# Seven half-block products for the last FFN group's down projection, and VectorE pieces of the first group in another order

## What is computed

```
x = x + gated_delta(layernorm(x))   # state S = beta*S + delta*k v^T per token, K = 64, V = 128
x = x + ffn(layernorm(x))
ffn(h):  hidden = sigmoid(h Q(w1)^T) * (h Q(w2)^T)     # 512 -> 1408
         return hidden Q(w3)^T                          # 1408 -> 512
Q(w) = clip(round(w / (mean|w| + 1e-8)), -1, 1)
```

## Time and profile before

| | |
|---|---|
| median of 3 runs | 318.64 us (318.29 to 318.87) |
| profiled execution, its own time | 318.46 us |
| its span, first to last instruction | 316.7 us |
| TensorE busy | 306.8 us, 97% |
| VectorE busy | 235.2 us, 74% |
| ScalarE busy | 183.2 us, 58% |
| GpSimd busy | 177.2 us, 56% |
| chain that ended last | TensorE 64%, VectorE 11%, ScalarE 6%, DMA 5%, GpSimd 4% |

### The profile page before, as it was taken

How to read it: one execution, slowest core, us unless ns; L and a number is a source line. 1 busy time by engine, 2 the same in 40 slices (tenths; PEclk the granted TensorE clock), 3 DMA queues, 4 the chain that set the end, 5 groups by cost and what they waited for, 6 DMA issues and landing times.

```text
span 316.7 us, 7197 instructions
## 1 busy us (share of the span) xinstructions
PE 306.8 (97%) x2548; PEld 213.2 (67%) x2548; DVE 235.2 (74%) x524; ACT 183.2 (58%) x413; POOL 177.2 (56%) x419
## 2 busy tenths in 40 slices
PE   7999999999999989999999999999999999999996
PEld 5888779874544434467888744778976448888545
DVE  6879989899989898897767879669677823455401
ACT  3587986969863673624666554346655406777200
POOL 7298325589993655997334896734467302444300
PEclk9999999999999999999999999999999999999999
DMA  6999900575862156630000039200000790000011
GB/s 180 380 387 395 398 24 0 67 135 100 129 108 50 34 85 133 103 99 17 3 3 0 3 64 211 91 2 2 3 2 0 90 245 33 3 0 2 2 66 66
DMA packets 55027, 29.43 MB, mean 93 GB/s; under 512 B 46800, under 2 KB 47568, under 8 KB 54992
## 3 DMA queue, kind: packets, MB, share of 16 engines
q1 hardware_dynamic: 54672, 28.97, 36.4%
q10 hardware_dynamic: 320, 0.00, 0.1%
HBM read 13.89 MB, written 4.19 MB: 57 GB/s over the span
## 4 chain that ended last, share of the span: by engine, by line
PE 64%; DVE 11%; ACT 6%; DMA 5%; issue 5%; POOL 4%; SPq 3%; DVEq 0%; POOLq 0%; ACTq 0%
PE ffn L1638 23%; PE ffn L1620 9%; PE pd L1638 8%; PE pd L1620 8%; PE ffn L1436 5%; DVE X L1125 3%; PE lev L1512 3%; DMA x_sb<-in_L_attn_x_dram 3%; PE pd L1446 2%; ACT q L793 2%; DMA w12T<-q 2%; SPq L404 2%; DVE sc L1187 2%; PE lev L1469 1%; ACT w12T L781 1%
## 5 line engine op out<-in xcount | busy, mean ns | idle before, releaser
L1638 PE MATMUL ffn<-w_nat,w12T 128*128 128x256 f16 x468 | 63.1, 273 | 0.0
L646 POOL TENSOR_TENSOR xnT<-xnT,q 128x256 f32<-128x256 f32 x33 | 24.3, 736 | 65.5 <-ACT xnT L975 45.0
L1638 PEld LDWEIGHTS ffn<-w_nat,w12T 128*128 128x128 f16 x468 | 45.1, 98 | 8.5 <-issue 1.5
L1620 PE MATMUL ffn<-w3T,w_nat 128*128 128x512 f16 x220 | 48.3, 379 | 0.0
L1591 PE MATMUL ffn<-w_nat,w12T 128*128 128x512 f16 x176 | 39.2, 379 | 2.3 <-DVE xnT L1330 2.3
L1620 PEld LDWEIGHTS ffn<-w3T,w_nat 128*128 128x128 f16 x220 | 21.6, 98 | 25.8 <-issue 0.6
L1638 PE MATMUL ffn<-w_nat 128*128 128x256 f16 x216 | 32.4, 273 | 0.0
L1591 PEld LDWEIGHTS ffn<-w_nat,w12T 128*128 128x128 f16 x176 | 16.9, 98 | 22.7 <-issue 3.8
L1436 PE MATMUL ffn<-xnT,w_proj 128*128 128x256 f32 x128 | 29.5, 384 | 1.2 <-ACT xnT L722 0.8
L1381 DVE TENSOR_TENSOR w_nat<-xnT,w_nat 128x512 f16<-128x512 f32 x33 | 23.1, 699 | 9.1 <-ACT w_nat L983 8.5
L1365 DVE SCALAR_TENSOR_TENSOR q<-ffn,w_nat 128x256 f32<-128x256 f32 x33 | 14.0, 424 | 21.0 <-PE ffn L1638 20.9
(11 more groups left out here) (194 smaller groups left out, 642.1 us busy)
## 6 DMA issues: line engine op xcount, KB each, us to landing
x_sb<-in_L_attn_x_dram SPq DMA_DIRECT2D x16, 256.0 KB, 8.3
out_dram<-x_sb SPq DMA_DIRECT2D x15, 256.0 KB, 2.1
w_nat<-in_L_ffn_w_dram SPq DMA_DIRECT2D x2, 1536.0 KB, 12.1
w_nat<-in_L_ffn_w_dram SPq DMA_DIRECT2D x2, 1408.0 KB, 15.5
w_nat<-in_L_ffn_w_dram SPq DMA_DIRECT2D x2, 1280.0 KB, 12.9
...
```

The source lines that it names most:

```text
L646: nc.gpsimd.tensor_tensor(hid32[:, u % 2, HP:2 * HP], sig[:, u % 2, HP:2 * HP], up[:, u % 2, HP:2 * HP], ALU.mult).then_inc(pool_hid, 1)
L1620: done = nc.tensor.matmul(down_bank(g, m)[:, :], hid_at(g, part, j, m), w3T[:, j, :], start=n == 0, stop=n == 2 * HT - 1)
L1638: done = nc.tensor.matmul(out[:, 0:HP], weights[:, t, u * P:(u + 1) * P], tokens[:, part, t, :], start=first and t == 0 and part == 0, sto ...
```

## The change

**Down projection of group 3.** Of the 11 hidden tiles ten are taken as two halves of five (JD = 5), the 512 tokens as two halves (the sequences b), the 512 output columns as two halves. The 2x2 by 2x2 block product is made from seven block products instead of eight, each of 20 matmuls of 256 columns (2 token tiles, 2 parts, 5 hidden tiles), and the eleventh tile adds 16 matmuls. `down_blocks` writes out their order on TensorE.

The factors that aren't there yet are made during the loop. GpSimd makes one difference or sum of 256 columns per step behind hidden_a, in steps for u = 0 to 9; VectorE makes four f16 weight differences of 1280 columns in steps k = 2 to 5 behind up_a, and two f32 pieces of 256 columns for each of five tiles (`down_sums`) between hidden_lo and up_a in steps k = 8 to 11 (two pairs in the last). The four sums are split into f16 parts by ScalarE (`down_hi_early`, `down_hi_late`) and VectorE (`down_lo`), 1280 columns each. VectorE adds each block product to x_sb as it is done (`down_group`), and SP stores in five parts (`store_blocks`). The first five hidden tiles are kept in f32 in buffers that are free by then (keep_at). The hidden scale of the last group is 16 instead of 64.

**First group.** In the tables of group 0, norm2 and apply of chunk 2 and its splits and transposes stand one unit later, and so do two weight sums. In `product1` the wait for y_ready of u = 1 is gone for group 1.

Left out below: new semaphores, hs(g) in place of HS, hid_f32 in place of hid32, `half_block` and `rest_block` (one matmul of 256 columns each; two for the eleventh tile), `add_block` (one scalar_tensor_tensor), and the removal of `down_last` and of the halves in `add_out` and `store_y`.

```diff
-    HS = 64.0
+    HS, HS_LAST = 64.0, 16.0
+    JD = (HT - 1) // 2
...
-        DVE_NEXT_FAST = {k: v for k, v in DVE_AFTER.items() if k != "xlo"}
-        DVE_NEXT_FAST |= {"sums": (None, 12), "xlo": (8, 12), "xloS": (None, 12)}
-        ACT_NEXT_FAST = {"gt": (2, 7), "oT": (4, 9), "xhiN": (7, 12), "xhiS": (8, 12)}
+        DVE_NEXT_FAST = {"chain0": (0, 5), "chain1": (0, 5), "masks": (2, 7), "state": (4, 9), "resid": (5, 11),
+                         "norm2": (6, 11), "apply": (7, 12), "sums": (None, 12), "xlo": (9, 12), "xloS": (None, 12)}
-        ACT_NEXT_FAST = {"gt": (2, 7), "oT": (4, 9), "xhiN": (7, 12), "xhiS": (8, 12)}
+        ACT_NEXT_FAST = {"gt": (2, 7), "oT": (4, 9), "xhiN": (8, 12), "xhiS": (9, 12)}
-        SP_NEXT_FAST = {"turn": (9, 12)}
+        SP_NEXT_FAST = {"turn": (10, 12)}
-        T_AT = {4: (3,), 5: (2,), 7: (4,), HT + 2: (1,)}
+        T_AT = {4: (3,), 6: (2,), 8: (4,), HT + 2: (1,)}
...
+        keep_at = ([xs[:, b, :, :].rearrange("p s d -> p (s d)").bitcast(f32) for b in range(B)]
+                   + [w_nat[:, WN + at:WN + at + 512] for at in (XS_AT[2][1] + 640, XS_AT[2][1] + 640 + 512, T_END)])
+        dsum = [f[:, 0:JD * HP].rearrange("p (j n) -> p j n", j=JD)
+                for f in (x_all[:, :, :, :].rearrange("p a b d -> p (a b d)"),
+                          x_all[:, :, :, :].rearrange("p a b d -> p (a b d)")[:, JD * HP:2 * JD * HP],
+                          X[:, :, :].rearrange("p l n -> p (l n)"),
+                          w_proj[:, :, :, :].rearrange("p a t n -> p (a t n)"))]
+        dsplit = store[:, :, :].rearrange("p c n -> p (c n)").bitcast(f16)[:, 0:8 * JD * HP].rearrange(
+            "p (n s j m) -> p n s j m", n=4, s=2, j=JD)
+        DT1, DT2, DT3, DT4 = (w_nat[:, WN + at:WN + at + JD * P].bitcast(f16).rearrange("p (j n) -> p j n", j=JD)
+                              for at in (0, JD * P, 2 * JD * P, XS_AT[2][1]))
+        d_left, d_right = slice(0, HP), slice(HP, D)
+        d_rows, d_rest = slice(0, JD), slice(JD, 2 * JD)
...
+            return keep_at[u] if g == G - 1 and u < JD else hid32[:, u % 2, :]
...
+            return {"x": pab[0][:, t * HP:(t + 1) * HP], "y": pab[1][:, t * HP:(t + 1) * HP],
+                    "v": pco[0][:, t * HP:(t + 1) * HP], "z": (pco[1], bank[0])[t][:, 0:HP]}[name]
...
+            def store_blocks(g):
+
+                sp_.wait_ge(y_ready, g * DT + 1)
+                store_half(0, d_left, slice(2 * g, 2 * g + 2))
+                sp_.wait_ge(x_read, 3)
+                store_half(1, d_left, slice(2 * g, 2 * g + 2))
+                sp_.wait_ge(y_ready, g * DT + 2)
+                store_half(0, d_right, slice(2 * g, 2 * g + 1))
+                sp_.wait_ge(y_ready, g * DT + 3)
+                store_half(1, d_right, slice(2 * g, 2 * g + 2))
+                sp_.wait_ge(y_ready, g * DT + 4)
+                store_half(0, d_right, slice(2 * g + 1, 2 * g + 2))
...
+                if g == G - 1 and u > JD + 1:
+                    pool.wait_ge(d24_ready, u - JD - 1)
+                nc.gpsimd.tensor_tensor(hid_f32(g, u)[:, 0:HP], sig[:, u % 2, 0:HP], up[:, u % 2, 0:HP],
                                         ALU.mult).then_inc(pool_hid, 1)
+                if g == G - 1 and u < JD:
+                    pool.wait_ge(pool_hid, 2 * n + 2)
+                    nc.gpsimd.tensor_tensor(dsum[2][:, u, :], hid_f32(g, u)[:, 0:HP], hid_f32(g, u)[:, HP:2 * HP],
+                                            ALU.subtract).then_inc(d3_ready, 1)
+                if g == G - 1 and JD <= u < 2 * JD:
+                    pool.wait_ge(pool_hid, 2 * n + 2)
+                    nc.gpsimd.tensor_tensor(dsum[0][:, u - JD, :], hid_f32(g, u - JD)[:, HP:2 * HP],
+                                            hid_f32(g, u)[:, HP:2 * HP], ALU.add).then_inc(d1_ready, 1)
...
+            def down_hi_early():
+
+                act.wait_ge(d24_ready, JD)
+                nc.scalar.activation(dsplit[:, 1, 0, :, :], dsum[1], ACT.Copy).then_inc(dhi_ready, 1)
+                act.wait_ge(d1_ready, JD)
+                nc.scalar.activation(dsplit[:, 0, 0, :, :], dsum[0], ACT.Copy).then_inc(dhi_ready, 1)
+
+            def down_hi_late():
+
+                act.wait_ge(d3_ready, JD)
+                nc.scalar.activation(dsplit[:, 2, 0, :, :], dsum[2], ACT.Copy).then_inc(dhi_ready, 1)
+                nc.scalar.activation(dsplit[:, 3, 0, :, :], dsum[3], ACT.Copy).then_inc(dhi_ready, 1)
...
+                    down_hi_early()
                 hidden_hi(g, HT - 1)
+                if g == G - 1:
+                    down_hi_late()
+                    return
...
+            def down_weights(n):
+
+                left, right = w3T[:, :, d_left], w3T[:, :, d_right]
+                if n == 0:
+                    done = nc.vector.tensor_tensor(DT3, right[:, d_rest, :], right[:, d_rows, :], ALU.subtract)
+                if n == 1:
+                    done = nc.vector.tensor_tensor(DT2, DT3, left[:, d_rows, :], ALU.add)
+                if n == 2:
+                    done = nc.vector.tensor_tensor(DT4, left[:, d_rest, :], DT2, ALU.subtract)
+                if n == 3:
+                    done = nc.vector.tensor_tensor(DT1, right[:, d_rows, :], left[:, d_rows, :], ALU.subtract)
+                done.then_inc(dT_ready, 1)
+                dve.wait_ge(dT_ready, n + 1)
+
+            def down_sums(g, p):
+
+                dve.wait_ge(d1_ready, p + 1)
+                dve.wait_ge(pool_hid, 2 * fast_n(g, JD + p) + 2)
+                link(nc.vector.tensor_tensor(dsum[1][:, p, :], dsum[0][:, p, :], hid_f32(g, p)[:, 0:HP], ALU.subtract))
+                nc.vector.tensor_tensor(dsum[3][:, p, :], hid_f32(g, JD + p)[:, 0:HP], dsum[1][:, p, :],
+                                        ALU.subtract).then_inc(d24_ready, 1)
+
+            def down_lo(n, nth):
+
+                dve.wait_ge(dhi_ready, nth)
+                nc.vector.tensor_tensor(dsplit[:, n, 1, :, :], dsum[n], dsplit[:, n, 0, :, :],
+                                        ALU.subtract).then_inc(dlo_ready, 1)
+
+            def add_block(g, b, cols, name, t=None):
+
+                if t is None:
+                    y = x_sb[:, b, 2 * g:2 * g + 2, cols]
+                    part = {"x": pab[0], "y": pab[1], "v": pco[0]}[name][:, :].rearrange("p (t n) -> p t n", t=2)
+                else:
+                    y = x_sb[:, b, 2 * g + t, cols]
+                    part = d_bank(name, t)
+                return nc.vector.scalar_tensor_tensor(y, part, 1.0 / HS_LAST, y, ALU.mult, ALU.add)
+
+            def down_group(g):
+
+                dve.wait_ge(dx_done, 1)
+                add_block(g, 0, d_left, "x").then_inc(x_read, 1)
+                down_lo(1, 1)
+                hidden_lo(g, HT - 1)
+                down_lo(0, 2)
+                dve.wait_ge(dx_done, 2)
+                add_block(g, 0, d_right, "x").then_inc(x_read, 1)
+                down_lo(2, 3)
+                dve.wait_ge(dy_done, 1)
+                dve.wait_ge(x_read, 1)
+                add_block(g, 0, d_left, "y").then_inc(y_ready, 1)
+                down_lo(3, 4)
+                dve.wait_ge(dz_done, 1)
+                for t in range(2):
+                    read = add_block(g, 1, d_right, "z", t)
+                read.then_inc(z_read, 1)
+                dve.wait_ge(dv_done, 1)
+                link(add_block(g, 1, d_left, "v"))
+                dve.wait_ge(dx_done, 3)
+                add_block(g, 1, d_left, "x").then_inc(x_read, 1)
+                dve.wait_ge(dz_done, 2)
+                dve.wait_ge(x_read, 2)
+                add_block(g, 0, d_right, "z", 0).then_inc(y_ready, 1)
+                dve.wait_ge(dx_done, 4)
+                dve.wait_ge(z_read, 1)
+                add_block(g, 1, d_right, "x").then_inc(y_ready, 1)
+                dve.wait_ge(dz_done, 3)
+                add_block(g, 0, d_right, "z", 1).then_inc(y_ready, 1)
...
+                    if g == G - 1 and JD <= k - 3:
+                        down_sums(g, k - 3 - JD)
+                    if g == G - 1 and k == HT:
+                        down_sums(g, JD - 1)
                     if k > 0:
                         up_a(g, k - 1)
+                    if g == G - 1 and 2 <= k < 6:
+                        down_weights(k - 2)
...
+            def down_blocks(g):
+
+                N = 4 * JD
+                left, right = w3T[:, :, d_left], w3T[:, :, d_right]
+                product5(g, HT - 1)
+                for n in range(4):
+                    half_block("x", plain(0, 0), left[:, d_rows, :], n, True)
+                product4(g, HT - 1)
+                for n in range(4, 12):
+                    half_block("x", plain(0, 0), left[:, d_rows, :], n, True)
+                product3(g, HT - 1)
+                for n in range(12, N):
+                    done = half_block("x", plain(0, 0), left[:, d_rows, :], n, True)
+                done.then_inc(dx_done, 1)
+                pe.wait_ge(hi_ready, g * HT + 2 * JD)
```

(46 more changed lines are left out.)

90 lines of the change are left out of this document (51 added, 39 removed).

## The result

| | changed kernel | kernel before, same job |
|---|---|---|
| first measurement, 4 runs each | 321.72 us (321.25 to 321.88) | 318.71 us (318.29 to 318.87) |
| again, beside the experiments | 321.24 us (320.53 to 321.58), 5 runs | 318.83 us, 15 runs |
| ratio, first measurement | 1.0089, 95% interval 1.0077 to 1.0101 | |
| ratio, again | 1.0072, 95% interval 1.0059 to 1.0084 | |
| profiled execution | 321.82 us, span 319.8 | 318.46 us, span 316.7 |

The change makes the kernel slower, by 2.4 to 3.0 us. The forecast was 0.7 us faster, 317.9, and the range ended at 319.9: wrong in sign and outside the range.

A forecast was written before the change was run, and what follows sets the result against it. TensorE's matmuls bound the end, a VectorE, GpSimd and ScalarE chain the first group. Terms -1.99 + 0.2 + 0.49 + 0.54 = -0.76, block times -0.9; with first group +0.2: -0.7, 317.9 us, range 316.8 to 319.9.

The forecast's parts named there:

- Columns: Last down projection on TensorE: fewer columns, 19.07 us before and 17.08 after, 1.99 saved if TensorE never waits.
- Rival 4: Down projection: narrow products don't save, going by the length of one instead of by columns; 321.5 us, chance 0.02.
- GpSimd's ten pieces: Last group's loop: ten extra 256-column pieces, 0.73 us each, hidden in GpSimd's idle time; cost 0.
- dropped y_ready wait: Group 1's product1(1, 1): the wait was worth 0.4 us, but VectorE's gapless work covers it; effect 0.
- Weight differences: Last group's loop, steps 2 to 5: VectorE's pieces make hidden_a late, counted twice in four steps; +0.2, bounds 0 and 0.45.
- Ring of sums: Loop steps 8 to 11: sums delay up_a, hidden_a, hidden_hi, next hidden_lo; 3.40 us a ring; +0.49, bounds 0.29 and 1.39.
- GpSimd's late grip: Loop's sums: GpSimd takes the shared port after its record's start, an argument against hidden_b (0.25) beating the second sum (0.38).
- Block four: Down projection: TensorE waits for the split of sum 2; +0.54, bounds 0.15 and 1.2.
- Tail: After the last matmul: a 256-column add and 128 KB store as now; 0, bounds 0 and 0.3.
- First group: Second weight sum can block GpSimd's sums, delaying split, signs and chunk 3's residual add: 0.9 gained to 1.2 lost; +0.2 taken.
- the block times: Down projection's end worked out block by block: 313.2 against 314.13, so -0.9 in place of the summed terms' -0.76.
- Rival 2: Last group: hidden_b always first at the shared port; ring 1.39, block waits 1.2, weights 0.45; 319.5 to 320.3, chance 0.25.

The follow-up runs named there:

- experiment 7: Down projection's half alone, weight differences moved into group 2, sums put behind up_a one step earlier, against the kernel before: 316.76 us, ratio 0.9939.
- experiment 11: Down projection's half alone, with GpSimd's ten additional pieces cut from 256 to 16 columns: 320.58 us.
- experiment 1: Kernel before with the first-group half of the change alone (tables, weight sum places, dropped y_ready wait): 319.36 us against 318.90, ratio 1.0018.
- 10: Kernel before with the first-group half alone and ScalarE's split of chunk 2's sums one unit later: 317.75 us, ratio 0.9965.
- experiment 5: The changed kernel measured again, unaltered, against the kernel before: 321.24 us, ratio 1.0072; its profiled run kept the full clock.

## Why the prediction was wrong, point by point

- *Columns, -1.99.* Right: -2.03 in experiment 7, where nothing waits. Rival 4 (narrow products that don't save, 321.5) came nearest to the measured time and is refuted by this.
- *GpSimd's ten pieces, 0; dropped y_ready wait, no cost seen; scale constants, 0.* Right for the first (experiment 11). The wait was only tried within experiments 1 and 10; its part in either was not separated.
- *Weight differences, +0.2 (bounds 0 and 0.45).* Measured 1.29 in the trace, three times the upper bound. The step that failed is "Chains of odd and even steps are separate, so this counts twice in four steps". They are not: in ScalarE's queue hidden_hi of one tile stands ahead of sigmoid_b of the next, for which that tile's hidden_b and hidden_a wait. So the port's 0.58 us, less the 0.21 to spare, is paid in every step, 0.37 each, and the step time goes up by it. The spare time that the prediction used, 0.39, is that of TensorE, not that of this path. The 0.6 of lateness for a piece was right, the 0.8 of its length alone too; that hidden_b would hold up the difference first (1.21) was not seen.
- *Ring of sums, +0.49 (bounds 0.29 and 1.39).* Measured 1.29 in the loop (2.55 less the 1.26 of the weight steps). The second sum takes 0.75 for 0.34; every other term of the 3.40 holds within 0.01. The failed step is the choice "I take 0.49, the order that lies between". Hidden_b was at the port 0.3 us before the second sum each time, as the prediction's own 0.25 against 0.38 said; GpSimd's late grip, put against it, shows in no record: each second sum ends 0.28 or 0.29 us after hidden_b.
- *Block four, +0.54.* Right in size: 0.42 of idle time by TensorE's list, 0.58 by the starts (303.79 + 2.19 against 306.56).
- *Tail, 0 (bounds 0 and 0.3).* 0.28 in the trace. From the last matmul to the end it is 4.46 to 4.69 us in all kernels with this down projection, 4.34 to 4.38 in the three without.
- *First group, +0.2.* At the full clock this came true, by the path that the prediction followed: the sums are blocked for 1.78 us (2.00 + 1.24 for 2 x 0.73; forecast 1.6), behind them come split, sign pieces, sigmoid and residual add, and the o product is 0.14 us late in the trace of experiment 5 (115.94 against 115.80) and the half 0.24 by the runs of experiment 1. Of the 1.78 us 1.27 are the weight sum's, the rest that of a hidden piece beside the fourth sum. What failed is that the sentence on what stands behind the split stopped at the residual add. It did not follow the sign pieces to SP's transposes of w3, 3.45 us long, and to TensorE at tiles 9 and 10. Queued work was counted as time only, not by who waits for what it writes. With that wait the clock falls in most runs and costs 0.6 to 0.9 us, a term that the sum has at nothing. Why it falls in some runs and not in others stays open.
- *Against the sum.* The prediction's terms with the first group's 0.2 make -0.56, which is 318.0; its 317.9 takes -0.9 from the block times in place of -0.76. Measured: last group -1.99 + 1.29 + 1.29 + 0.58 leaves 1.17 of the measured 1.31, the tail 0.28, the first group 1.08, and 0.71 by which the profiled execution of before lay early.
- *Rivals.* Rival 2, the port lost each time, is what happened in the loop, with the price that it names for the ring. It ended at 320.3 because it took 0.45 for the weights, 0.84 too little, and had no term for the clock.
